# First attention on one Trainium2 core: a pair's two heads in the two halves of the array's rows

## The reference, cut to what matters

```python
# x: (2, 1024, 256); 16 heads of 16 columns, so 32 (batch, head) pairs in all
q, k, v = proj(Wq), proj(Wk), proj(Wv)            # (B, H, S, dh)
q, k = _apply_rope(q, cos, sin), _apply_rope(k, cos, sin)
scores = einsum('bhqd,bhkd->bhqk', q, k) / sqrt(dh)
scores = where(causal, scores, finfo(float32).min)
probs = softmax(scores, axis=-1)
attn = einsum('bhqk,bhkd->bhqd', probs, v)        # then @ Wo.T
```

## Time and profile before

| what | value |
|---|---|
| median of three runs | 1616.67 us |
| profiled execution | 1620.91 us |
| its span, first to last instruction | 1618.9 us |
| first attention, first score matmul to last value copy | 105.05 to 394.98 us |
| mean granted TensorE clock over the span | 0.936 |
| busy over the span: PE, DVE, ACT, POOL | 88%, 65%, 51%, 23% |

### The profile page before, as it was taken

One profiled execution on the slowest core, in us unless ns is written; L12 is line 12 of the kernel. 1 busy time (PEld: TensorE's weight loads), 2 busy tenths in 40 slices (PEclk: granted clock), 3 DMA queues, 4 the chain that ended last, 5 costly groups with the idle time before them and its releaser, 6 DMA issues. The chain is left out here.

```text
span 1618.9 us, 36474 instructions
## 1 busy us (share of the span) xinstructions
PE 1427.8 (88%) x12900; PEld 999.5 (62%) x12901; DVE 1052.0 (65%) x2181; ACT 820.9 (51%) x1692; POOL 374.2 (23%) x796
## 2 busy tenths in 40 slices
PE   3848999998669999999889999999998798699979
PEld 2414555454546666677677666767767645599954
DVE  4857677674768888888822888888882368422236
ACT  1216655555127777777720777777771115332330
POOL 0445565520111111111110111111101000477720
PEclk9969999999779999999999999999999889799975
DMA  3038999961026555555620665555552340599957
GB/s 97 1 65 178 250 249 239 206 137 28 1 76 118 129 135 133 125 135 122 133 63 1 119 136 127 134 133 127 133 118 46 97 122 0 152 281 291 280 165 233
DMA packets 463400, 215.07 MB, mean 133 GB/s; under 512 B 412082, under 2 KB 434448, under 8 KB 463072
## 3 DMA queue, kind: packets, MB, share of 16 engines
q1 hardware_dynamic: 448992, 175.09, 45.6%
q0 software_dynamic: 12000, 36.90, 7.8%
q10 hardware_dynamic: 2336, 2.16, 0.4%
HBM read 81.97 MB, written 31.52 MB: 70 GB/s over the span
## 5 line engine op out<-in xcount | busy, mean ns | idle before, releaser
L1053 PE MATMUL bank<-a_pt,v_part 128*128 128x128 f16 x3456 | 235.9, 221 | 40.2 <-DVE z_part L1143 26.4
L1053 PEld LDWEIGHTS bank<-a_pt,v_part 128*128 128x128 f16 x3456 | 208.1, 98 | 74.7 <-issue 32.2
L1124 DVE TENSOR_REDUCE a_negm<-bank 128x1 f32<-128x1024 f32 (+7 forms) x256 | 192.5, 752 | 84.6 <-PE bank L1037 84.4
L737 DVE TENSOR_REDUCE a_qh<-bank 128x1 f16<-128x1024 f32 (+7 forms) x256 | 182.4, 755 | 86.2 <-PE bank L627 84.5
L1032 PE MATMUL bank<-a_k,a_q 128*128 128x512 f16 (+3 forms) x1152 | 228.7, 326 | 0.2
L1116 ACT ACTIVATE a_ph<-a_p,a_rinv 128x1024 f16<-128x1024 f32 (+7 forms) x256 | 198.2, 775 | 56.4 <-POOL a_rinv L995 51.9
L725 ACT ACTIVATE a_p<-bank 128x1024 f32<-128x1024 f32 (+7 forms) x256 | 158.0, 649 | 129.6 <-PE bank L682 113.4
L1158 DVE SCALAR_TENSOR_TENSOR a_ph<-a_p,a_rinv,a_ph 128x1024 f16<-128x1024 f32 (+7 forms) x256 | 207.1, 809 | 1.7 <-ACT a_ph L1116 1.7
L995 POOL TENSOR_TENSOR a_rinv<-a_rinv,p_scale 128x1 f32<-128x1 f32 x256 | 48.8, 191 | 646.3 <-DVE a_rinv L1137 646.1
L1105 ACT ACTIVATE a_p<-bank,a_negm 128x1024 f32<-128x1024 f32 (+7 forms) x256 | 188.9, 738 | 5.0 <-DVE a_negm L1124 4.9
L904 PE MATMUL bank<-x_part,wsplit 128*128 128x512 f16 x768 | 187.4, 381 | 4.0 <-PEq L188 1.8
(11 more groups left out here) (206 smaller groups left out, 2277.3 us busy)
## 6 DMA issues: line engine op xcount, KB each, us to landing
wgu<-in_wgu SPq DMA_DIRECT2D x64, 352.0 KB
choice_rows<-zero POOLq DMA_DIRECT2D x24, 512.0 KB, 5.0
c_rows<-choice_rows SPq DMA_DIRECT2D x16, 768.0 KB, 11.3
wsplit<-w_parts POOLq DMA_DIRECT2D x30, 384.0 KB, 3.9
wd<-in_wd SPq DMA_DIRECT2D x64, 176.0 KB
pw_in<-in_wqkv SPq DMA_DIRECT2D x16, 384.0 KB, 5.5
w_parts<-pw_part SPq DMA_DIRECT2D x16, 384.0 KB, 2.9
a_pt<-a_ph SPq DMA_TRANSPOSE x256, 2.9
```

The lines of the kernel that those rows point to most:

```text
L737: dve.tensor_reduce(qh[s][:, i, MC:MC + 1], s1_place(t), AX.X, ALU.max, negate=True).then_inc(m_ready, 1)
L1053: ins = eng.matmul(Z_ps[:, cols], g.vs[par][v_][:, k, :], turned[slot][:, a * blocks[j] + k, :], start=(k == 0 and (v_, a) == PARTS[0]), s ...
L1124: eng.tensor_reduce(negm[:, par, j:j + 1], S_ps[j % 4][:, 0:blocks[j] * P], AX.X, ALU.max, negate=True).then_inc(m_ready, 1)
```

## The change

A pair's two heads now share one operand: head 0 in columns 0 to 63, head 1 in 64 to 127, each with three products of 16 (48 columns; low by low is left out) and its own maximum column. After the transposes head 0 lies in partitions 0 to 63 and head 1 in 64 to 127, and each score matmul contracts over 64 rows: one half of the array's rows. One set of transposes serves both heads; the column pass has its own copy of the keys, `kTb`.

The passes go in pieces of at most 512 columns (one bank): 12 per head and pass, 24 per pair and pass, alternating between the heads. Each pass has three places of one bank. `scores(col, row)` issues a column piece of one half and a row piece of the other half, of the same width, one after the other. The causal mask comes in two matmuls of 64 rows per diagonal piece; `swapped` holds identity and mask with the halves exchanged, loaded and cast at the start. A row of more than 512 keys has two partial maxima in `half`; two small reductions per pair combine them.

SP and POOL work per pair instead of per head, with two weight jobs and two zero stores per pair.

```diff
+    swapped = np.roll(np.stack([ident, mask], 1), P // 2, axis=0)
...
+                sp.dma_start(swapf[:, :, :], g.t["c_swapped"]).then_inc(s_c, 16)
...
+                dve.tensor_copy(g.swapped[:, :, :], swapf[:, :, :]).then_inc(s_v, 1)
...
-    MC = 4 * DH0
...
+    MC = 3 * DH0
...
-    SESSIONS = {1: (0, 1, 2), 3: (3, 4), 7: (5, 6), 9: (7, 8, 9)}
-    ZT_STEP, TURN_STEP, Z_STEP = 11, 13, 15
-    ORDER = (0, 7, 1, 6, 2, 5, 3, 4)
-    EARLY = 6
+    SESSIONS = {2: (0, 1, 2), 6: (3, 4), 10: (5, 6), 14: (7, 8, 9)}
+    ZT_STEP, TURN_STEP, Z_STEP = 16, 19, 21
+    ROWS = ((6, 0), (4, 1), (5, 0), (5, 1), (7, 1), (2, 0), (7, 0), (0, 0), (3, 0), (1, 0), (4, 0), (6, 1))
+    COLS = ((0, 0), (7, 0), (0, 1), (6, 0), (1, 0), (5, 0), (2, 0), (3, 1), (3, 0), (2, 1), (4, 0), (1, 1))
+    NC_ = len(ROWS)
+    NS = 2 * NC_
+    NB_ = 3
+    EARLY = 11
...
+        kTb = [g.sb(f"a0_kb{i}", [P, S], F16, c) for i in range(2)]
...
-        ST = [g.bank[0].rearrange("p a n -> p (a n)"), g.bank[1][:, 0, :]]
-        S1 = [g.bank[2].rearrange("p a n -> p (a n)"), g.bank[1][:, 1, :]]
+        half = g.sb("a0_half", [P, 2, 2, BT // 2, 2], F32, c)
+        ST = [g.bank[0][:, 0, :], g.bank[0][:, 1, :], g.bank[1][:, 0, :]]
+        S1 = [g.bank[2][:, 0, :], g.bank[2][:, 1, :], g.bank[1][:, 1, :]]
...
+        def row_piece(t):
+            i, c4 = ROWS[(t + 1) // 2 % NC_]
+            return t % 2, i, 4 * c4, min(4, i + 1 - 4 * c4)
+        def col_piece(k):
+            kb, c4 = COLS[k // 2]
+            return k % 2, kb, kb + 4 * c4, min(4, BT - kb - 4 * c4)
...
+        def halves(h):
+            at = slice(h * HP, (h + 1) * HP)
+            pairs = ((g.identb[at, :], g.maskb[at, :]), (g.swapped[at, 0, :], g.swapped[at, 1, :]))
+            return pairs if h == 0 else pairs[::-1]
...
+                    q = qh[m % 2].rearrange("p t (h c) -> p h t c", h=2)
+                    k = kh[m % 2].rearrange("p t (h c) -> p h t c", h=2)
+                    done = w_in[m % 2]
+                    src = g.qk[:, 2 * m:2 * m + 2, :, :, :]
+                    pool.tensor_copy(q[:, :, :, 0:2 * DH0], src[:, :, :, 0, :]).then_inc(done, 1)
+                    pool.tensor_copy(q[:, :, :, 2 * DH0:MC], src[:, :, :, 0, 0:DH0]).then_inc(done, 1)
+                    pool.tensor_copy(k[:, :, :, 0:DH0], src[:, :, :, 1, 0:DH0]).then_inc(done, 1)
+                    pool.tensor_copy(k[:, :, :, DH0:MC], src[:, :, :, 1, :]).then_inc(done, 1)
+                    pool.memset(q[:, :, :, MC:MC + 1], 0.0).then_inc(done, 1)
...
-                for m in range(4, NH):
+                for m in range(2, NP):
                     fetch(m)
                     fetch_values(m - 2)
-                    if m - 4 < WJOBS:
-                        w_split(pool, m - 4)
-                    if m - 4 < ZD:
-                        pool.dma_start(zv[m - 4], g.zero[:, :]).then_inc(g.s_zero, 16)
+                    for q in (2 * m - 4, 2 * m - 3):
+                        if q < WJOBS:
+                            w_split(pool, q)
+                        if q < ZD:
+                            pool.dma_start(zv[q], g.zero[:, :]).then_inc(g.s_zero, 16)
...
+                def turn_keys(m):
+                    if m >= 2:
+                        sp.wait_ge(st_ready, (m - 1) * NS)
+                    sp.dma_start_transpose(kTb[m % 2].rearrange("p (t n) -> p t n", n=P),
+                                           kh[m % 2].rearrange("p t d -> p (t d)")).then_inc(tm_in[m % 2], 16)
...
+                for m in range(NP):
+                    sp.wait_ge(c_ready, 2 * m + 2)
                     if m >= 2:
-                        sp.wait_ge(st_ready, (m - 1) * BT)
-                    sp.dma_start_transpose(qmT[m % 2][:, :, :], qh[m % 4].rearrange("p t d -> p (t d)")
-                                           ).then_inc(tm_in[m % 2], 16)
-                    if m + 2 < NH:
+                        sp.wait_ge(st_ready, (m - 1) * NS)
+                    sp.dma_start_transpose(qmT[m % 2].rearrange("p (t n) -> p t n", n=P),
+                                           qh[m % 2].rearrange("p t d -> p (t d)")).then_inc(tm_in[m % 2], 16)
+                    if m + 2 < NP:
                         turn(m + 2)
-                    if 0 <= m - 3 < WJOBS:
-                        w_store(sp, m - 3)
-                        if m - 1 < WJOBS:
-                            w_load(sp, m - 1)
+                    if m + 1 < NP:
+                        turn_keys(m + 1)
+                    for q in (2 * m - 2, 2 * m - 1):
+                        if 0 <= q < WJOBS:
+                            w_store(sp, q)
+                    for q in (2 * m, 2 * m + 1):
+                        if 2 <= q < WJOBS:
+                            w_load(sp, q)
...
+                def scores(col, row):
+                    if col is not None:
+                        k, m, par, at_start = col
+                        hc, kb, q0, nc_ = col_piece(k)
+                        if k == 0:
+                            pe.wait_ge(tm_in[par], m * 16 + (32 - 16 * par))
+                        if not (at_start and k < NB_):
+                            pe.wait_ge(e_ready, m * NS + (k - NB_ + 1))
+                        at = slice(hc * HP, (hc + 1) * HP)
+                        cs = ST[k % NB_]
+                        c_diag = q0 == kb
+                        ci = pe.matmul(cs[:, 0:nc_ * P], kTb[par][at, kb * P:(kb + 1) * P],
+                                       qmT[par][at, q0 * P:(q0 + nc_) * P], start=True, stop=not c_diag)
+                    if row is not None:
+                        t, m, par, at_start = row
+                        hr, i, k0, nr_ = row_piece(t)
+                        if t == 0:
+                            pe.wait_ge(t_in[par], m * 16 + (32 - 16 * par))
+                        if not (at_start and t < NB_):
+                            pe.wait_ge(m_ready, m * NS + (t - NB_ + 1))
+                        at = slice(hr * HP, (hr + 1) * HP)
+                        rs = S1[t % NB_]
+                        r_diag = k0 + nr_ == i + 1
+                        ri = pe.matmul(rs[:, 0:nr_ * P], qT[par][at, i * P:(i + 1) * P],
+                                       kT[par][at, k0 * P:(k0 + nr_) * P], start=True, stop=not r_diag)
+                    for x in range(2):
+                        if col is not None and c_diag:
+                            ident, mask = halves(hc)[x]
+                            ci = pe.matmul(cs[:, x * HP:(x + 1) * HP], mask, ident[:, x * HP:(x + 1) * HP],
+                                           start=False, stop=x == 1)
+                        if row is not None and r_diag:
+                            ident, mask = halves(hr)[x]
+                            ri = pe.matmul(rs[:, (nr_ - 1) * P + x * HP:nr_ * P], ident, mask[:, x * HP:P],
+                                           start=False, stop=x == 1)
+                    if col is not None:
+                        ci.then_inc(st_ready, 1)
+                    if row is not None:
+                        ri.then_inc(s1_ready, 1)
...
+                def maximum(t, m, par):
+                    dve.wait_ge(s1_ready, m * NS + (t + 1))
+                    h, i, k0, n_ = row_piece(t)
+                    if i >= BT // 2:
+                        dve.tensor_reduce(half[:, par, h, i - BT // 2, k0 // 4:k0 // 4 + 1], S1[t % NB_][:, 0:n_ * P],
+                                          AX.X, ALU.max).then_inc(m_ready, 1)
+                    else:
+                        dve.tensor_reduce(qh[par][:, i, h * HP + MC:h * HP + MC + 1], S1[t % NB_][:, 0:n_ * P],
+                                          AX.X, ALU.max, negate=True).then_inc(m_ready, 1)
+                    if t >= NS - 2:
+                        dve.wait_ge(m_ready, m * NS + (t + 1))
+                        dst = qh[par][:, BT // 2:BT, h * HP + MC:h * HP + MC + 1].rearrange("p t o -> p (t o)")
+                        dve.tensor_reduce(dst, half[:, par, h, :, :], AX.X, ALU.max, negate=True).then_inc(c_ready, 1)
```

More of the change, by code:

```diff
@@ L524, in _ @@
             def _(pool):
-                for i in range(4):
-                    pool.memset(qh[i][:, :, MC:P], 0.0).then_inc(s_pre, 1)
                 for i in range(2):
[L529 to L533, removed]
+                    cols = qh[i].rearrange("p t (h c) -> p t h c", h=2)
@@ L559, in _ @@
+                    pool.tensor_copy(vh[m % 2][:, :, :, 0:DH0], g.v0[:, 2 * m:2 * m + 2, :, :]).then_inc(v_in, 1)
                 zv = g.krows.rearrange("(z p n) d -> z p (n d)", p=P, z=ZD)
-                for m in range(4):
-                    fetch(m)
-                    if m >= 2:
-                        fetch_values(m - 2)
+                fetch(0)
+                fetch(1)
                 w_begin(pool)
-                for m in range(4, NH):
+                for m in range(2, NP):
                     fetch(m)
@@ L575, in _ @@
+                fetch_values(NP - 2)
+                fetch_values(NP - 1)
```

(39 more changed lines are left out.)

164 lines of the change are left out of this document (56 added, 108 removed).

## The result

The changed kernel takes 1625.56 us, median of 5 runs (1622.58 to 1626.77); the kernel before, beside it, 1616.67 (1613.95 to 1617.43, 5 runs). The ratio is 1.0048 [1.0031, 1.0064]: slower, by 8.9 us where 11 were forecast, and inside the range. The profiled execution took 1626.46 us with a span of 1624.8; it is 0.9 above its median, where the one of before was 4.2 above.

A forecast was written before the change was run, and what follows sets the result against it. An SP, DMA and POOL loop bounds the changed kernel: start 135, 7 x 20.9 + 4 x 17.0 gives 349.3, then transposes, 29 and 17.5 put the last values at 400.9; +11 us, 1628 on the median, range 1606 to 1640.

The forecast's parts named there:

- The loop closes within one pair and holds TensorE: SP, DMA and POOL: load, two splits, fetch and transposes follow without overlap; 20.9 us a turn against 14.5 of computing.
- The signs: Trace after: POOL waits 5 to 6 us once a pair, TensorE 5 to 6 for transposes; clock falls, DMA share 0.7 to 0.8.
- A large turn: One turn of the SP and POOL loop with large weight jobs: 11.5 + 7.5 + 1.9 = 20.9 us, 7 turns.
- the first one, 11.5: From SP's first transpose to the start of POOL's split: 10.3 us plus 1.2 for a second store in front of the load.
- A small turn: One turn of the loop with 256 KB jobs: 10.3 + 4.8 + 1.9 = 17.0 us, 4 turns.
- rival 2: SP and POOL loop turns faster: 1 us less a turn is no change, 2 less 1606 us; chance 0.15, plus 0.11 near break-even.
- The start: Start of the stage: first exp near 121.2 us, qmT landing 3.5 us, `fetch(3)` ending near 135.
- 14.5 us of computing a pair: A pair without the loop: VectorE's 13.4 us plus half of the old 2.3 us of waits.
- VectorE's floor: VectorE's work a pair: maxima 11.4, division 1.4, two small reductions 0.6; 13.4 us.
- The halves overlap: TensorE's column and row pieces run beside each other: 10.7 us a pair, against 15.1 if they do not.
- rival 1: Array halves do not overlap: TensorE needs 15.1 us and keeps its waits, 17 us a pair; 1634 to 1640 us; chance 0.13.
- The constant `swapped`: 128 KB loaded ahead of x in the queue: 0.5 us, an estimate from x's 2 MB.

The follow-up runs named there:

- run above: Changed kernel with each pair's two weight loads ahead of its two stores, both still behind the transposes; 1623.37 us, ratio to the kernel before 1.0037.
- loads first: Changed kernel with SP issuing each pair's two stores and two weight loads ahead of its key and query transposes; 1595.05 us, ratio to the kernel before 0.9871.
- The runs with one half: Row pieces put in the same array half as the step's column piece: 1631.91 us in the changed kernel, 1614.24 with stores and loads ahead of transposes.
- the kernel before with loads first: Kernel before the change, with a head's store and load issued ahead of its transposes; 1626.5 us, ratio 1.0060.

## Why the prediction was right, point by point

1. *The loop closes within one pair and holds TensorE.* Shown: by SP's and POOL's rows, by 2.3 us of memsets that cost 2.2 a turn, and by the loop's going when SP's order alone was changed. The signs came as foretold: one wait of POOL a pair and none at the second load, TensorE's waits for a transpose (0.5 to 4.3 us, 5 to 6 foretold), clock below 1.00, DMA share 0.67 to 0.75. Only POOL's wait is 10 us and not 5 to 6: it begins where the fetch ends, so it is the whole landing.
2. *A large turn, 20.9 us.* It took 19.9. The term that was too big is the first one, 11.5: the seven took 9.5 to 11.9, mean 10.3. The second store did cost some 1.1 (run above), but the rest was about as much shorter, with DMA engines no longer full and the zero stores issued outside that stretch; no run separates these two reasons. -7.2 us over 7 turns. Splits (7.5) and fetch (1.8 to 1.9) were right.
3. *A small turn, 17.0 us.* 16.0: -4.1 over four. So all eleven turns were 1 us shorter than forecast. That is the mechanism of rival 2 at its own break-even, where 1 us less a turn was to be no change.
4. *The start.* `fetch(3)` ended at 140.1 and not 135: +5.1. The first exp came at 124.75, not 121.2 (the row below, which answers to the earlier trace rows): the maxima of pair 0 were ready at 119.3, not 117.7, and eleven row pieces of pair 1, which stand in TensorE's program before the first column piece, held that one to 123.94, 1.4 us after qmT had landed. And qmT of pair 1 took 6.1 us to land (132.23 to 138.29), not 3.5.

```profile
124.75 1.25 ACT L775 ACTIVATE a_p<-bank 128x512 f32<-128x512 f32 x3 [25.97 <-PE bank L727]
```

5. *14.5 us of computing a pair.* At full clock it was 14.8 with loads first, and VectorE's floor was nearly right (13.1 us busy a pair, 13.4 foretold), though TensorE was as busy (13.2). What the forecast did not price is the clock: it foretold that the clock would fall, but put no time on it, and a pair at 0.90 takes 1.5 us more. Behind `fetch(14)` (343.0, 349.3 foretold) the changed kernel needed 56.4 us to its last values instead of 51.6: +4.8. The granted clock is 0.92 there; by the 1.5 us of a pair at 0.90 that is some 4 of the 4.8, an estimate. Adding up the steps: 5.1 - 7.2 - 4.1 + 4.8 = -1.4, and the last values start at 399.40 instead of 400.9:

```profile
399.40 5.37 PE L675 MATMUL bank<-a_p,a_vh 128*17 128x256 f32 x80 [1.01 <-ACT a_p L775]
```

They take 1.3 us longer than in the earlier trace rows, with a granted clock of 0.81 from 396 to 405 us: the same missing term.

6. *The halves overlap* (rival 1 against it). They do, at the full rate. The forecast priced it at 15.1 - 10.7 = 4.4 us a pair of TensorE's time. The runs with one half took away part of that, and cost 1.0 us a pair at full clock; they do not test the 4.4.
7. *The constant `swapped`.* +0.7 at the start of the batch statistics (0.5 foretold).

So the cause was right: with the loop taken out the kernel is 21 us faster than before. That the total came near was luck, as errors of 4 to 7 us in four terms cancelled. The sign owes something to it too: with the turns as they were and the other terms as forecast, the sum would have been no change, and what made the kernel slower beyond that is mainly the late start and the clock at the end.

## What to carry to other kernels

When two iterations become one, look for every chain that closed over two of them: a load issued behind a transpose, which waits for a copy, which stands behind the work on the load before, costs its whole length as soon as it fits into one iteration, though each engine in it is half idle. The remedy is in the order of the queue: what waits for nothing new goes ahead of what waits, and here that turned 8.9 us of loss into 21 of gain. And an engine's saving is smaller than its columns say: from before to loads first, both at full clock, a pair lost 4.0 us of TensorE's columns by the forecast's count, 2.9 of its busy time (16.1 to 13.2) and 2.2 of its length (17.0 to 14.8), with VectorE busy 13.1 of what is left; then the lower clock took back 0.9 on average.

## What the runs showed of the hardware that was not expected

- In every run with half-array scores the granted clock over the stage was below 1.00, though single pairs ran at 1.00: 0.94 with TensorE busy 54.6 us of 60 (loads first), where full-array scores at 57.0 of 60 had 1.00, and at 53.7 of 60 in the kernel before with loads first still 1.00.
- Two matmuls in different halves of the rows start 0.01 us apart and keep the full rate: with their masks they are 640 and 704 columns, 0.28 to 0.30 us by the 0.43 ns a column of the earlier trace rows, and the next piece in the same half starts 0.29 and 0.31 us after the first.
- Two 384 KB stores ahead of a load on the same queue cost the load some 1.1 us each here, and a store behind two loads lands 5.7 us after its issue instead of 3.2 (medians, 140 to 320 us): order on a queue moves the cost between them.
- A further session of values between scores costs 0.22 us, of it 0.12 where pairs of the same granted clock are compared; two sessions of 40 values instead of four of 16 to 24 cost 27 us, with ScalarE waiting up to 4.1 us behind one.
